# Edge stage of a graph network: low product at 128 weight columns, casts on ScalarE, source one-hots seven at once

## What is computed

```python
def _sage_layer(x, src, dst, deg_inv, Wl, bl, Wr):
    agg = jax.ops.segment_sum(x[src], dst, num_segments=n) * deg_inv
    h = agg @ Wl.T + bl + x @ Wr.T
    norm = jnp.maximum(jnp.linalg.norm(h, axis=-1, keepdims=True), EPS)
    return jax.nn.relu(h / norm)

h = _sage_layer(x, src, dst, deg_inv, Wl0, bl0, Wr0)
h = _sage_layer(h, src, dst, deg_inv, Wl1, bl1, Wr1)
```

## Time and profile before

| | us |
|---|---|
| median of 3 runs | 8597.83 |
| lowest and highest | 8597.27, 8611.64 |
| the profiled execution's own time | 8560.43 |
| its span, first to last instruction | 8558.7 |
| mean granted TensorE clock | 0.792 of full speed |
| TensorE busy | 7549.9 |
| POOL busy | 5709.4 |
| VectorE busy | 5075.6 |
| ScalarE busy | 2669.4 |

### The profile page before, as it was taken

The page is one execution under the profiler, slowest core; times in us unless marked ns, Lnnn a source line. Parts: engine busy times, 40 slices in busy tenths (PEclk is TensorE's granted clock), DMA queues, the critical chain, the costliest instruction groups (busy, mean ns, idle before and its releaser), DMA issues. The chain is left out here.

```text
span 8558.7 us, 155389 instructions
## 1 busy us (share of the span) xinstructions
PE 7549.9 (88%) x39416; PEld 5082.7 (59%) x39416; DVE 5075.6 (59%) x19374; ACT 2669.4 (31%) x5404; POOL 5709.4 (67%) x4866
## 2 busy tenths in 40 slices
PE   5888888898898888988898988899999979999994
PEld 4777777787777777877787776432323342222222
DVE  5777777677777533333333333577777757777774
ACT  2222222222222222222222223444444454444443
POOL 5888888778888888888788883255555545455553
PEclk7777777667777767676767676799999969999995
DMA  4333333233333222222222222200000020000001
GB/s 121 35 34 34 34 34 34 33 33 34 34 34 34 30 27 28 27 27 27 27 27 27 27 27 72 58 18 18 18 18 18 18 54 18 17 18 18 18 18 48
DMA packets 652909, 272.68 MB, mean 32 GB/s; under 512 B 544598, under 2 KB 600314, under 8 KB 652360
## 3 DMA queue, kind: packets, MB, share of 16 engines
q0 software_dynamic: 325280, 163.91, 17.5%
q1 hardware_dynamic: 326500, 105.06, 5.6%
q10 hardware_dynamic: 900, 1.60, 0.1%
HBM read 189.59 MB, written 80.61 MB: 32 GB/s over the span
## 5 line engine op out<-in xcount | busy, mean ns | idle before, releaser
L651 POOL DMA_INDIRECT future<-sbuf,sidx x1564 | 2512.0, 1606 | 526.9 <-issue 452.4
L637 POOL DMA_INDIRECT gbuf<-in_x_dram,gidx x1564 | 1565.4, 1001 | 482.4 <-issue 469.8
L1441 ACT CAST dense<-bank 128x512 bf16<-128x512 f32 x2072 | 1207.4, 586 | 1493.6 <-PE bank L1458 1211.3
L1345 POOL DMA_INDIRECT gb<-h,nidx x728 | 703.5, 966 | 721.9 <-DVE at_dst L1376 524.6
L1345 POOL DMA_INDIRECT gb<-x,nidx x728 | 704.0, 967 | 711.1 <-DVE at_dst L1376 519.0
L1468 PE MATMUL bank<-dense,wide 128*128 128x512 bf16 x2744 | 1055.2, 385 | 138.5 <-DVE dense L1412 99.4
L1458 PE MATMUL bank<-at_dst,at_src 128*128 128x512 bf16 x2744 | 1069.6, 393 | 68.5 <-DVE at_dst L1376 68.5
L1469 PE MATMUL bank<-dense,wide 128*64 128x512 bf16 x2744 | 1117.7, 407 | 0.0
L1376 DVE TENSOR_SCALAR at_dst<-iota,metaf 128x512 bf16<-128x512 f16 x2758 | 988.3, 358 | 0.0
L1469 PEld LDWEIGHTS bank<-dense,wide 128*64 128x64 bf16 x2744 | 292.1, 106 | 1156.1 <-issue 1156.1
L1374 DVE TENSOR_SCALAR at_src<-iota,metaf 128x128 bf16<-128x128 f16 x2758 | 727.2, 264 | 323.6 <-PE bank L1458 264.2
(11 more groups left out here) (255 smaller groups left out, 11781.3 us busy)
## 6 DMA issues: line engine op xcount, KB each, us to landing
gbuf<-in_x_dram,gidx POOLq DMA_INDIRECT x1564
comb<-in_edge_attr_dram SPq DMA_DIRECT2D x391, 64.0 KB
future<-sbuf,sidx POOLq DMA_INDIRECT x1564
blkb<-blkrow SPq DMA_DIRECT2D x210, 98.0 KB
future<-zero POOLq DMA_DIRECT2D x16, 800.0 KB, 17.7
fut<-future SPq DMA_DIRECT2D x100, 125.0 KB
gb<-x,nidx POOLq DMA_INDIRECT x732, 2.4
gb<-h,nidx POOLq DMA_INDIRECT x732, 2.4
```

What stands on the lines that cost most here:

```text
L637: pool.indirect_dma_start(out=gbuf[:, b, q, :], out_offset=None, in_=x[:, :], in_offset=bass.IndirectOffsetOnAxis(ap=gidx[:, b, q:q + 1], ...
L651: pool.indirect_dma_start(out=future[q][:, :], out_offset=bass.IndirectOffsetOnAxis(ap=sidx[:, b, q:q + 1], axis=0), in_=sbuf[:, b, q, :], ...
L1345: pool.indirect_dma_start(out=gb1[:, m, q, :], out_offset=None, in_=frm[:, :], in_offset=bass.IndirectOffsetOnAxis(ap=nidx[:, m, q:q + 1], ...
L1441: act.copy(dense[:, b % AR, :], psA[b % AR][:, :]).then_inc(t_cpA, 1)
```

## The change

The product with the low third takes 128 weight columns: it begins at the low third of block b and runs on over the high third of block b + 1, so that rows 64 to 127 of `psL` hold something that nothing reads. Behind the last block 64 columns of zeros are appended. ScalarE makes all 98 casts. The source one-hots of 7 blocks are made by one compare of two tensors (`sources`), in two halves of `at_src`; the destination one-hots stay one by one (`destinations`). The semaphores `t_cpA` and `t_cpD` become one `t_cp`; `t_end` tells of the zeros.

```diff
--- before.py
+++ after.py
@@ -122,7 +122,8 @@
 
         wide = sb("wide", [P, NW])
         cnt = wide[0:D, :]
-        pieces = wide[:, 0:BLOCKS * XPCS * D // 2].bitcast(BF16).rearrange("p (b k) -> p b k", b=BLOCKS)
+        parts16 = wide[:, 0:(BLOCKS * XPCS + 1) * D // 2].bitcast(BF16)
+        pieces = parts16[:, 0:BLOCKS * XPCS * D].rearrange("p (b k) -> p b k", b=BLOCKS)
 
 
         ident = sb("ident", [P, P])
@@ -1273,8 +1274,6 @@
             at = same.index(m)
             return same[at - 1] - (POOLG if at == 0 else 0)
 
-        DVE_COPIES = [b for b in range(BLOCKS) if b % 4 == 3]
-        ACT_COPIES = [b for b in range(BLOCKS) if b % 4 != 3]
         ADDS = POOLG + 3
 
         for layer in range(2):
@@ -1282,7 +1281,7 @@
             gb1 = tmp(f"gb{layer}", [P, POOLG, TILES, D])
             nidx = tmp(f"nidx{layer}", [P, POOLG, TILES], I32)
             xf = tmp(f"xf{layer}", [P, 3, XB, D])
-            at_src = tmp(f"at_src{layer}", [P, RING, P], BF16)
+            at_src = tmp(f"at_src{layer}", [P, 2, RING, P], BF16)
             at_dst = tmp(f"at_dst{layer}", [P, RING, SPAN], BF16)
             dense = tmp(f"dense{layer}", [P, AR, SPAN], BF16)
             metaf = tmp(f"metaf{layer}", [P, 2, BLOCKS])
@@ -1311,8 +1310,8 @@
             t_metaf = lsem("metaf")
             t_at = lsem("at")
             t_A = lsem("A")
-            t_cpA = lsem("cpA")
-            t_cpD = lsem("cpD")
+            t_cp = lsem("cp")
+            t_end = lsem("end")
             t_ap = lsem("ap")
             t_ms = lsem("ms")
 
@@ -1360,6 +1359,7 @@
                     dve.wait_ge(t_prep, 3)
                     dve.tensor_scalar(base[:, 0:PEG], base0[:, 0:PEG], -float(W), None, ALU.add)
 
+                    dve.memset(parts16[:, BLOCKS * XPCS * D:(BLOCKS * XPCS + 1) * D], 0.0).then_inc(t_end, 1)
                     for c in range(BLOCKS // XB):
                         own_b = slice(c * XB, (c + 1) * XB)
                         dve.wait_ge(t_hi, c + 1)
@@ -1369,10 +1369,13 @@
                         dve.tensor_tensor(pieces[:, own_b, 2 * D:3 * D], xf[:, c % 3, :, :], pieces[:, own_b, D:2 * D],
                                           ALU.subtract).then_inc(t_x, 1)
 
-                    def one_hots(i, b):
-
-                        dve.tensor_scalar(at_src[:, b % RING, :], iota16[:, 0:P], metaf[:, 0, b:b + 1], None,
+                    def sources(k):
+
+                        dve.tensor_tensor(at_src[:, k % 2, :, :], iota16[:, 0:P].unsqueeze(1).to_broadcast([P, RING, P]),
+                                          metaf[:, 0, k * RING:(k + 1) * RING].unsqueeze(2).to_broadcast([P, RING, P]),
                                           ALU.is_equal)
+
+                    def destinations(b):
                         dve.tensor_scalar(at_dst[:, b % RING, :], iota16[:, :], metaf[:, 1, b:b + 1], None,
                                           ALU.is_equal).then_inc(t_at, 1)
 
@@ -1399,8 +1402,9 @@
                         add_window(at, psG[SUM_SLOT[m]][0:D, 0:W], W, i, m)
 
                     places_of(0)
+                    sources(0)
                     for b in range(RING):
-                        one_hots(0, b)
+                        destinations(b)
                     with dve.Fori(0, SBS) as i:
                         indices(POOLG * i + PEG, HALVES, POOLG)
                         for b in range(BLOCKS):
@@ -1408,12 +1412,12 @@
                                 if b == TAKE[m] - 5:
                                     compare(i, m)
                             dve.wait_ge(t_A, BLOCKS * i + (b + 1))
-                            if b in DVE_COPIES:
-                                dve.tensor_copy(dense[:, b % AR, :], psA[b % AR][:, :]).then_inc(t_cpD, 1)
                             if b == BLOCKS - RING:
                                 dve.wait_ge(t_at, BLOCKS * i + BLOCKS)
                                 places_of(i + 1)
-                            one_hots(i, (b + RING) % BLOCKS)
+                            if b % RING == 0:
+                                sources((b // RING + 1) % (BLOCKS // RING))
+                            destinations((b + RING) % BLOCKS)
                             for m in range(POOLG):
                                 if b == TAKE[m] + 2:
                                     add_sums(i, m)
@@ -1436,9 +1440,9 @@
                         act.wait_ge(t_rest, c + 1)
                         act.copy(pieces[:, own_b, D:2 * D], xf[:, c % 3, :, :]).then_inc(t_mid, 1)
                     with act.Fori(0, SBS) as i:
-                        for b in ACT_COPIES:
+                        for b in range(BLOCKS):
                             act.wait_ge(t_A, BLOCKS * i + (b + 1))
-                            act.copy(dense[:, b % AR, :], psA[b % AR][:, :]).then_inc(t_cpA, 1)
+                            act.copy(dense[:, b % AR, :], psA[b % AR][:, :]).then_inc(t_cp, 1)
                         act.wait_ge(t_acc, ADDS * i + ADDS)
                         act.wait_ge(t_ap, BLOCKS * i + BLOCKS)
                         act.copy(midsum[:, :], psHM[D:2 * D, :]).then_inc(t_ms, 1)
@@ -1447,26 +1451,23 @@
                 def _(pe):
                     pe.sem_inc(t_S, POOLG)
 
-                    def copied(i, b):
-                        if b in DVE_COPIES:
-                            pe.wait_ge(t_cpD, len(DVE_COPIES) * i + (DVE_COPIES.index(b) + 1))
-                        else:
-                            pe.wait_ge(t_cpA, len(ACT_COPIES) * i + (ACT_COPIES.index(b) + 1))
-
                     def adjacency(i, b):
                         pe.wait_ge(t_at, BLOCKS * i + (b + 1))
-                        pe.matmul(psA[b % AR][:, :], at_src[:, b % RING, :], at_dst[:, b % RING, :],
+                        pe.matmul(psA[b % AR][:, :], at_src[:, (b // RING) % 2, b % RING, :], at_dst[:, b % RING, :],
                                   start=True, stop=True).then_inc(t_A, 1)
 
                     def apply(i, b):
-                        copied(i, b)
+                        pe.wait_ge(t_cp, BLOCKS * i + (b + 1))
                         if b == 0:
                             pe.wait_ge(t_acc, ADDS * i + (ADDS - 1))
                             pe.wait_ge(t_ms, i + 1)
-                        if b % XB == 0:
-                            pe.wait_ge(t_x, b // XB + 1)
+                        if b == 0:
+                            pe.wait_ge(t_x, 1)
+                            pe.wait_ge(t_end, 1)
+                        if b % XB == XB - 1 and b < BLOCKS - 1:
+                            pe.wait_ge(t_x, b // XB + 2)
                         pe.matmul(psHM[:, :], pieces[:, b, 0:2 * D], dense[:, b % AR, :], start=(b == 0), stop=(b == BLOCKS - 1))
-                        pe.matmul(psL[0:D, :], pieces[:, b, 2 * D:3 * D], dense[:, b % AR, :],
+                        pe.matmul(psL[:, :], parts16[:, (b * XPCS + 2) * D:(b * XPCS + 4) * D], dense[:, b % AR, :],
                                   start=(b == 0), stop=(b == BLOCKS - 1)).then_inc(t_ap, 1)
 
                     def sums(i, m):
```

## The result

The changed kernel takes 8383.45 us (median of 4 runs, 8373.33 to 8389.63), the kernel before beside it 8597.55. The ratio is 0.9746, interval 0.9729 to 0.9763: 214 us gained where 602 were forecast, and outside the range given.

The account below looks back on a forecast made before the run. TensorE was taken to bound the edge loops; superblocks falling from 97.4 and 99.8 to 77.1 us, times 14, save 284 + 318 = 602 us, giving a median of 7996, range 7930 to 8125.

Parts of the forecast that it names:

- What bounds the kernel: Edge loops: TensorE bounds; the two steps where product width changes between 128 and 64 are long, block 0.87 us.
- Rival 2: Edge loops: width is not the reason, body stays 91.4 us, only the turn gains; 8480 us, chance 0.05.
- Part 1: Edge loops: all three products 128 wide, block 0.648 us, net 19.1 us saved a superblock, body 72.3.
- Part 2: Edge loops: ScalarE's 98 casts stay hidden, latency 1.08 us against 1.30; turn waits of 2.6 and 4.4 us go.
- its sign of being wrong: Edge loops: a block comes out over 0.70 us with TensorE waiting for ScalarE.
- The casts of VectorE: Superblock turn: TensorE no longer waits for a VectorE cast; 2.6 and 4.4 us go.
- Part 3: VectorE in edge loops: seven source one-hots in one compare, 1.08 us busy, hidden except at the turn.
- What is late next: Superblock turn: chain through VectorE to gathers stalls TensorE 1.8 us before the second group of gathered products.
- The way back to the loop top: VectorE's loop top: gap shrinks to 0.2 us in both layers, instead of staying at 2.4 and 4.5.
- Rival 1: VectorE's loop top: its gap stays and counts in full, 91 us; 8087 us, chance 0.25.
- Rival 3: Edge loops: POOL becomes the bound, held out by VectorE's compares; 8330 to 9140 us; chance 0.06 short of slower, 0.02 slower.

Follow-up runs that it names:

- early_deep: Changed kernel plus idle instructions before VectorE's loop, gathers allowed ten blocks earlier, four adjacency tiles, products three blocks behind, two gathered-sum tiles: ratio 0.9662.
- deep_pad: Changed kernel plus idle instructions before VectorE's loop, four adjacency tiles, products three blocks behind, two gathered-sum tiles, gathers not earlier: ratio 0.9631, median 8232.29 us.

## Why the prediction was wrong

- **What bounds the kernel, and why the low product was slow** (by width): right. With all three widths 128 the steps are 0.216; with the low product at 64, the other two parts in, they are those of before. Rival 2 is out.
- **Part 1, 19.1 us a superblock**: the sum of the steps was right, and is there once the gathers are gone (74.6 to 76.0 us a superblock; forecast 77.1, with 3.3 us at the turn that did not come). Beside the gathers it brings a fraction.
- **Part 2, the step that failed.** "The cast starts 0.43 after its product ... It fits by 0.2 us." That latency was taken from one undisturbed block of a TensorE with gaps, and treated as a constant. It is 0.416 in most blocks, over 0.7 in more than one waiting cast of five, and up to 3.6 us. The text itself gave the price: what is missing comes off each block; and its sign of being wrong, TensorE waiting for ScalarE, is what the rows show. The trace of before had a sign of it, the 62 late ones away from the turn and the 34 bursts. With the gathers replaced, layer 1 gains 1162.4 - 969.3 = 193 us over 13 superblocks, 14.8 each. TensorE's waits in the rows above and some of a few us together account for 180.1 - 21.4 = 159 of them (97 for casts, 48 ahead of gathered products), the clock of 0.99 for about 12; some 20 are not accounted for.
- **The casts of VectorE** no longer hold TensorE at the turn, and ScalarE does 98 in 0.587 each: right.
- **Part 3**: 1.09 us measured, 1.08 forecast. That it is hidden was not quite right: of the gathers, 235 overlap a long compare by over 0.5 us and are as a mean 0.44 us over the usual 0.95, those without overlap 0.02. That is 103 us of GpSimd in all, seen by TensorE only where the second gathered group waits.
- **What is late next**: the second gathered group was named, for 1.8 us; it is 4.2 us a superblock in layer 0 and 2.5 in layer 1, since gathers were taken at 1.26 apart and some last over 2.
- **The way back to the loop top**: taken as vanishing in both layers; it stays in layer 0 (2.30 us, 3.3 us a superblock with what it delays) and vanishes in layer 1. The rule of the Trainium skill (Runtime: NRT & Kernel Launch, Instruction fetch mechanics), two blocks of 256 instructions, gave "fits" for both, and the measurement decides against it here. See below.
- **Rival 1** held for one layer, some 46 us. **Rival 3** had the right engine and the wrong way to act: GpSimd is not the bound by its own time (in layer 1 it is busy for 701 us, with 0.30 between two of 674 gathers 903, of 1162), and does its harm to other engines' signals. By its time, 8330, it came nearest, by luck.

In numbers: 14 x (15.6 + 12.3) = 391 us, the distance of the superblocks from 77.1, are the 388 us by which the median misses. The ends of the range were rounded outward: the prediction's terms give 7941 and 8115, where it has 7930 and 8125; the result lies outside either.

## What to carry to other kernels

A slack of 0.2 us between engines, read from one block, is no slack: look at the distribution of the latency from product to follower over the whole trace, and at what else runs where it has a tail. Before TensorE is made denser beside indexed gathers of GpSimd, replace these for one run by plain copies; if that gives the forecast time and the gathers don't, signals are late. Here a third block of slack then bought 0.6%, and an earlier start of the gathers nothing. And where an engine stands for 2 us for no semaphore at a loop's top, move the loop by some idle instructions before it is rewritten.

## What was not expected of the hardware

- A signal of a TensorE product can reach ScalarE and VectorE, both idle, up to 3.2 us late, both at once (up to 6.1 in early_deep), while the recorded signals of the other engines come within 0.013. It took 52 indexed gathers per superblock and a TensorE without gaps: none late with 13 or 26 gathers, none with 52 plain copies from SyncE or GpSimd, 59 with 52 gathers and TensorE at 0.87 us a block, 375 (deep_pad) to 636 with 52 gathers at 0.65, whatever their bytes or rows.
- An indexed gather of 128 rows of 256 bytes occupies GpSimd for 0.95 us at least, of 64-byte rows as long, of 64 rows 0.05 less as a mean; a plain copy of 128 rows 0.56.
- VectorE's code comes in packets of 8192 bytes, and the fetches lie 128 instructions apart, so 64 bytes each (queue q14: 109 packets, 0.88 MB on the page; 201 and 1.65 MB before). The loop of 364 instructions lies over four such pieces in layer 0 of the changed kernel and is fetched again on every trip (at its instructions 71, 199 and 326, and at the top); in layer 1 it lies over three and is not fetched again. Padded so that it lies over three in both layers, it is fetched in neither. One case each, but by it the limit for a loop without fetches is three pieces of 128.
